# Inputs, expert rows and output in 4 KB runs per partition, and unread matmuls in TensorE's first idle time

## The reference

```python
def _fastmax_causal_p1(q, k, v):          # 16 heads of 64
    qn = jnp.max(jnp.linalg.norm(q, axis=-1), axis=-1)[..., None, None]
    kn = jnp.max(jnp.linalg.norm(k, axis=-1), axis=-1)[..., None, None]
    q = LIM * q / qn
    k = LIM * k / kn
    kv = jnp.cumsum(k[..., :, None] * v[..., None, :], axis=2)
    num = A0 * jnp.cumsum(v, axis=2) + A1 * jnp.einsum('bhnd,bhnde->bhne', q, kv)
    ksum = jnp.cumsum(k, axis=2)
    den = A0 * jnp.arange(1, n + 1) + A1 * jnp.einsum('bhnd,bhnd->bhn', q, ksum)
    return num / den[..., None]
# attention: vh @ Wo.T + bo
# experts: 8 of them, hidden width 352, top 2 per token, weights renormalised
acts = jax.nn.silu(gate) * up
expert_out = jnp.einsum('btef,efd->bted', acts, down_proj)
x = x + attention + jnp.einsum('bted,bte->btd', expert_out, expert_w)
```

## Time and profile before

| | |
|---|---|
| median of 3 runs | 1610.43 us (1609.39 to 1611.0) |
| profiled execution, its span | 1610.3 us |
| profiled execution, its own time | the span, with nothing else recorded around it: 0.13 us under the median |
| PE busy | 91% of the span |
| instructions | 39161 |
| DMA traffic | 53.44 MB, mean 33 GB/s |

### The profile page before, as it was taken

The page is one execution under the profiler, slowest core; times in us unless marked ns, Lnnn a source line. Parts: engine busy times, 40 slices in busy tenths (PEclk is TensorE's granted clock), DMA queues, the critical chain, the costliest instruction groups (busy, mean ns, idle before and its releaser), DMA issues.

```text
span 1610.3 us, 39161 instructions
## 1 busy us (share of the span) xinstructions
PE 1463.3 (91%) x9330; PEld 1317.9 (82%) x9332; DVE 1180.1 (73%) x3304; ACT 876.2 (54%) x2000; POOL 911.2 (57%) x1257
## 2 busy tenths in 40 slices
PE   2999975999999999999999999999998699999960
PEld 2999964888888888888888888888887699999960
DVE  7999997777777777777777777777777655555532
ACT  2999973555555555555555555555455444444430
POOL 3200016776776776776776776776676455555544
PEclk7999996999999999999999999999999899999985
DMA  9000000000000000000000000000000122222229
GB/s 289 19 0 0 0 1 14 12 11 8 11 11 8 11 11 8 11 11 8 11 11 8 11 11 8 11 11 8 10 11 7 42 63 62 61 63 62 59 65 291
DMA packets 72171, 53.44 MB, mean 33 GB/s; under 512 B 7840, under 2 KB 67360, under 8 KB 72096
## 3 DMA queue, kind: packets, MB, share of 16 engines
q1 hardware_dynamic: 54560, 28.95, 7.0%
q0 software_dynamic: 9216, 19.17, 3.4%
q10 hardware_dynamic: 8320, 4.19, 0.9%
HBM read 28.33 MB, written 23.96 MB: 32 GB/s over the span
## 4 chain that ended last, share of the span: by engine, by line
issue 31%; POOL 30%; PE 29%; POOLq 4%; DVE 3%; SPq 1%; DMA 1%; ACT 0%; DVEq 0%; ACTq 0%
POOL Al L414 11%; PE ybank L1248 6%; PE bank L1037 5%; PE bank L1039 5%; PE bank L1038 5%; POOL sorted_tokens L408 4%; POOL Ml L396 3%; POOL ysum L424 3%; PE ybank L1241 3%; POOL Mt L388 2%; POOL Mh L394 2%; SPq L331 1%; POOL xa L426 1%; PE ybank L1037 1%; PE ybank L1038 1%
## 5 line engine op out<-in xcount | busy, mean ns | idle before, releaser
L414 POOL TENSOR_TENSOR Al<-Am,Ah 128x512 fp32r<-128x512 f32 x256 | 329.4, 1287 | 177.7 <-ACT Ah L615 170.9
L615 ACT ACTIVATE Ah<-Am 128x512 fp32r<-128x512 f32 x256 | 161.5, 631 | 334.0 <-DVE Am L873 334.0
L1153 PE MATMUL ybank<-Wx,zf 128*128 128x129 f32 x2072 | 276.5, 276 | 4.8 <-ACT zf L620 4.8
L1153 PEld LDWEIGHTS ybank<-Wx,zf 128*128 128x128 f32 x2072 | 261.0, 191 | 22.3 <-issue 12.8
L866 DVE SCALAR_TENSOR_TENSOR ul<-bank,uh 128x512 fp32r<-128x512 f32 x256 | 174.0, 690 | 90.7 <-ACT uh L609 81.8
L898 DVE SCALAR_TENSOR_TENSOR acc<-ybank,rden,acc 128x128 f32<-128x128 f32 x780 | 217.7, 341 | 0.1
L504 POOL DMA_INDIRECT expert_rows<-yt,wdi x136 | 132.1, 972 | 142.0 <-ACT yt L687 121.5
L873 DVE TENSOR_TENSOR Am<-bank,causal 128x512 f32<-128x512 f32 x256 | 174.6, 682 | 23.1 <-PE bank L1039 23.1
L609 ACT ACTIVATE uh<-bank 128x512 fp32r<-128x512 f32 x256 | 148.7, 593 | 72.1 <-PE bank L1039 65.7
L786 DVE TENSOR_REDUCE ssq<-sq 128x448 f32 (+1 forms) x320 | 168.6, 573 | 7.6 <-ACT sq L557 5.8
L620 ACT ACTIVATE zf<-bank 128x512 f32<-128x512 f32 x258 | 151.7, 588 | 39.9 <-PE bank L1039 39.1
(11 more groups left out here) (225 smaller groups left out, 3906.2 us busy)
## 6 DMA issues: line engine op xcount, KB each, us to landing
xt<-sorted_tokens SPq DMA_DIRECT2D x137, 66.0 KB
er<-expert_rows SPq DMA_DIRECT2D x16, 512.0 KB, 8.5
xa<-in_L_attn_X SPq DMA_DIRECT2D x8, 512.0 KB, 7.3
out<-ot ACTq DMA_DIRECT2D x8, 512.0 KB, 7.1
expert_rows<-yt,wdi POOLq DMA_INDIRECT x136
sorted_tokens<-pay,sidx POOLq DMA_INDIRECT x128
gu<-in_L_ffn_gate_proj SPq DMA_DIRECT2D x1, 1408.0 KB
gu<-in_L_ffn_up_proj SPq DMA_DIRECT2D x1, 1408.0 KB
```

What stands on the lines that cost most here:

```text
L414: pool.tensor_tensor(Al[:, q], Am[:, q % 2], Ah[:, q], ALU.subtract).then_inc(e_Al, 1)
L615: act.activation(Ah[:, q], Am[:, q % 2], ACT.Copy).then_inc(e_Ah, 1)
L1153: last = pe.matmul(ybank[q % 2][:, i // 2, VE * (i % 2):VE * (i % 2) + VE], zf[:, q % 2, i, :], Wx[:, HQ * q + i, :], start=True, stop=True)
```

## The change

The host now lays out the inputs, and the kernel gives the output in another order, which the host turns back.

- x, wq, wk and wv come as [partition, tile, 128], so that each partition reads one run of 4 KB. `xa`, `wqn`, `wkn` and `wvn` hold the same values in the same places as before.
- gate and up come as one array, one run of 22 KB per partition and one DMA in place of two. The down weights come in two DMAs in place of sixteen, with `dn` laid out as [P, FT, E, D].
- `meta`'s destination rows change. The token in tile c of its batch at partition p now goes to row p*8 + c of the batch's block in `expert_rows`. The loads of `er` read the block with partition p taking rows 8p to 8p+7, a run of 4 KB. The scatters still write rows of 512 B, at other places.
- The output is [8, 128, 8, 128], a run of 4 KB per partition.
- PE gets `part_trials()` between the SETUP transpositions and its wait for their copies: 45 matmuls on zeros whose results nobody reads, some on 64 or 32 rows or columns of the array. POOL zeroes their two operands (2 memsets of 512 floats).

```diff
+        trial_r, trial_f = place("trial_r", [P, 4 * P], f32r), place("trial_f", [P, 4 * P])
...
-        dn = place("dn", [P, E, FT, D])
+        dn = place("dn", [P, FT, E, D])
...
             for n, (t, src) in enumerate(((wqn, wq), (wkn, wk))):
-                sp.dma_start(t[:], src.rearrange("(t p) d -> p t d", p=P)).then_inc(w_in[n], 16)
+                sp.dma_start(t[:], src).then_inc(w_in[n], 16)
             for n in range(8):
                 sp.dma_start(xa[:, 1 + n * CB:1 + (n + 1) * CB, :],
-                             x[n].rearrange("(c p) d -> p c d", p=P)).then_inc(x_in[n], 16)
-            sp.dma_start(wvn[:], wv.rearrange("(t p) d -> p t d", p=P)).then_inc(w_in[2], 16)
-            sp.dma_start(won[:], wo.rearrange("o (t d) -> o t d", d=D)).then_inc(w_in[3], 16)
+                             x[n]).then_inc(x_in[n], 16)
+            sp.dma_start(wvn[:], wv).then_inc(w_in[2], 16)
+            sp.dma_start(won[:], wo).then_inc(w_in[3], 16)
...
-            sp.dma_start(gu[:, :, 0, :], gate.rearrange("e d f -> d e f")).then_inc(f_w, 16)
-            sp.dma_start(gu[:, :, 1, :], up.rearrange("e d f -> d e f")).then_inc(f_w, 16)
+            sp.dma_start(gu[:], gate_up_w).then_inc(f_w, 16)
             sp.wait_ge(f_dz, 1)
-            for e in range(E):
-                sp.dma_start(dn[:, e, 0:2, :], down[e, 0:256, :].rearrange("(t p) d -> p t d", p=P)).then_inc(f_dn, 16)
-                sp.dma_start(dn[0:F - 256, e, 2, :], down[e, 256:F, :]).then_inc(f_dn, 16)
+            sp.dma_start(dn[:, 0:2], down_head).then_inc(f_dn, 16)
+            sp.dma_start(dn[0:F - 2 * P, 2], down_tail).then_inc(f_dn, 16)
...
-                        sp.dma_start(er[:, s, k], ys_d[bass.ds((b + B * k) * N, N), :].rearrange("(c p) d -> p c d", p=P)
+                        sp.dma_start(er[:, s, k], ys_d[bass.ds((b + B * k) * N, N), :].rearrange("(p c) d -> p c d", p=P)
...
-            pool.memset(dn[:, :, FT - 1, :], 0.0).then_inc(f_dz, 1)
+            pool.memset(dn[:, FT - 1], 0.0).then_inc(f_dz, 1)
+            pool.memset(trial_r[:].bitcast(f32), 0.0).then_inc(s_trial, 1)
+            pool.memset(trial_f[:], 0.0).then_inc(s_trial, 1)
...
-            pool.iota(meta[:, :, :, 0], pattern=[[P, C], [B * N, K2]], base=0, channel_multiplier=1,
+            pool.iota(meta[:].rearrange("p (b c) k m -> p b c k m", b=B)[:, :, :, :, 0],
+                      pattern=[[N, B], [1, CB], [B * N, K2]], base=0, channel_multiplier=CB,
...
-                    act.dma_start(out[bass.ds(b * CB, CB)].rearrange("c p d -> p c d"), ot[:, s]).then_inc(o_out[s], 16)
+                    act.dma_start(out[bass.ds(b, 1)].rearrange("a p c d -> p (a c) d"), ot[:, s]).then_inc(o_out[s], 16)
...
             for j, (kind, n) in enumerate(SETUP):
                 transpose4(bank[j], kind, n).then_inc(s_tr, 1)
+
+            def part_trials():
+
+                pe.wait_ge(s_trial, 2)
+                for n in range(6):
+                    pe.matmul(bank[4 + n % 4][:], trial_r[:, 0:P], trial_r[:], start=True, stop=True)
+                for n in range(6):
+                    pe.matmul(bank[4 + n % 4][:, 0:P], trial_r[:, 0:P], trial_r[:, 0:P], start=True, stop=True)
+                for rows in (64, 32):
+                    for n in range(8):
+                        t = slice(rows * n % P, rows * n % P + rows)
+                        pe.matmul(bank[4 + n % (P // rows)][:], trial_r[t, 0:P], trial_r[t, :], start=True, stop=True)
+                pe.matmul(bank[4][:], trial_f[:, 0:P], trial_f[:], start=True, stop=True)
+                for cols in (64, 32):
+                    for n in range(4):
+                        t = slice(cols * n % P, cols * n % P + cols)
+                        pe.matmul(bank[5][t, :], trial_f[:, t], trial_f[:], start=True, stop=True)
+                for n in range(4):
+                    r, c = slice(64 * (n % 2), 64 * (n % 2) + 64), slice(64 * (n // 2), 64 * (n // 2) + 64)
+                    pe.matmul(bank[6 + n % 2][c, :], trial_f[r, c], trial_f[r, :], start=True, stop=True)
+                for n in range(4):
+                    r = slice(64 * (n % 2), 64 * (n % 2) + 64)
+                    pe.matmul(bank[6 + n % 2][:, 0:P], trial_f[r, 0:P], trial_f[r, 0:P], start=True, stop=True)
+
+            part_trials()
             pe.wait_ge(s_trh, len(SETUP))
...
-            pe.wait_ge(f_dn, 32 * E)
+            pe.wait_ge(f_dn, 32)
```

More of the change, by code:

```diff
@@ L27 @@
+import numpy as np
 import concourse.bass as bass
@@ L52, with build @@
 EPS = 1e-5
-def build(nc, x, wq, wk, wv, wo, bo, rw, gate, up, down, out):
+def build(nc, x, wq, wk, wv, wo, bo, rw, gate_up_w, down_head, down_tail, out):
     f32, f32r, bf16 = mybir.dt.float32, mybir.dt.float32r, mybir.dt.bfloat16
@@ L195, in build @@
         s_stat, s_chain, s_rt, s_sqrt = sem("s_stat"), sem("s_chain"), sem("s_rt"), sem("s_sqrt")
-        s_rw = sem("s_rw")
+        s_rw, s_trial = sem("s_rw"), sem("s_trial")
         n_xn, n_xT, n_xTh, n_xTl = sem("n_xn"), sem("n_xT"), sem("n_xTh"), sem("n_xTl")
@@ L672, in _ @@
             barrier(act, 2)
-            act.wait_ge(f_w, 32)
+            act.wait_ge(f_w, 16)
             for e in (*range(E - 3, E), *range(E - 3)):
@@ L1247, in down_ @@
                 for t in range(FT):
-                    last = pe.matmul(bank[6 + s][:, 0:D], aT[:, s, t, :], dn[:, bass.ds(ex, 1), t, :].rearrange("p a f -> p (a f)"),
+                    last = pe.matmul(bank[6 + s][:, 0:D], aT[:, s, t, :], dn[:, t, bass.ds(ex, 1), :].rearrange("p a f -> p (a f)"),
                                      start=(t == 0), stop=(t == FT - 1))
@@ L1278, in _, with laid_out, a, by_partition @@
             barrier(pe, 3)
-_INS = ["L0_attn_X", "L0_attn_Wq", "L0_attn_Wk", "L0_attn_Wv", "L0_attn_Wo", "L0_attn_bo",
-        "L0_ffn_router_w", "L0_ffn_gate_proj", "L0_ffn_up_proj", "L0_ffn_down_proj"]
+def laid_out(inputs):
+    def a(name):
+        return np.asarray(inputs["L0_" + name])
+    def by_partition(w):
+        return w.reshape(8, P, D).transpose(1, 0, 2)
+    down = a("ffn_down_proj")
+    return {
+        "x": a("attn_X").reshape(B, CB, P, D).transpose(0, 2, 1, 3),
+        "wq": by_partition(a("attn_Wq")),
+        "wk": by_partition(a("attn_Wk")),
+        "wv": by_partition(a("attn_Wv")),
+        "wo": a("attn_Wo").reshape(D, 8, D),
+        "bo": a("attn_bo"),
+        "rw": a("ffn_router_w"),
+        "gate_up_w": np.stack([a("ffn_gate_proj"), a("ffn_up_proj")], axis=1).transpose(2, 0, 1, 3),
+        "down_head": down[:, :2 * P].reshape(E, 2, P, D).transpose(2, 1, 0, 3),
+        "down_tail": down[:, 2 * P:].transpose(1, 0, 2),
+    }
 def kernel(**inputs):
-    import numpy as np
     import concourse.bacc as bacc
@@ L1292 @@
     arrays, args = {}, []
-    for name in _INS:
-        a = np.ascontiguousarray(inputs[name])
+    for name, a in laid_out(inputs).items():
+        a = np.ascontiguousarray(a)
         arrays[f"in_{name}"] = a
         args.append(nc.dram_tensor(f"in_{name}", a.shape, mb.dt.from_np(a.dtype), kind="ExternalInput").ap())
-    args.append(nc.dram_tensor("out_0", (C, P, D), mb.dt.float32, kind="ExternalOutput").ap())
+    args.append(nc.dram_tensor("out_0", (B, P, CB, D), mb.dt.float32, kind="ExternalOutput").ap())
     build(nc, *args)
     r = run(nc, [arrays], core_ids=[0])
-    return r.results[0]["out_0"].reshape(B, N, D)
+    return np.ascontiguousarray(r.results[0]["out_0"].transpose(0, 2, 1, 3)).reshape(B, N, D)
```

## The result

The change makes the kernel slightly slower. The median is 1612.93 us (19 executions, 1610.29 to 1618.57) against 1610.05 us for the kernel before on the same chips (19 executions, 1608.23 to 1612.48): a ratio of 1.0018, 95% interval 1.0011 to 1.0026. The forecast was 1602.3 us, with a range of 1599.0 to 1606.5.

A forecast was written before the change was run, and what follows sets the result against it. DMA was taken to bound the last stage and DVE the first 33 us; -6.8 (output), -0.5 (last store), -0.8 (front) and 0 (trials) gave -8.1 us, 1602.3 us, range 1599.0 to 1606.5.

The forecast's parts named there:

- the trials at nothing: PE's first idle time: the 45 unread matmuls fit in 18.4 us of idleness and change the total by 0.
- The front: Start of the kernel: wqn's load lands earlier in larger packets, gaining 0.8 us, bounded by 0 and 1.5.
- DVE never waits again: Front: after wqn lands DVE works without a gap, so earlier landing of other loads gains nothing.
- the output stage: Last stage, DMA bound: 11.3 MB at 400 GB/s gains 6.8 us, the last store 0.5 us more.
- rival (2): Output stage: a data ceiling at 370 GB/s cuts the gain to 4.6 us, total 1604.6 us; chance 0.13.
- SP waiting for a buffer with the DMA idle: Output stage: a sign, named beforehand, that would show the forecast wrong; no size given.
- the round trip: Output stage: a buffer's adds, hand-overs and load take 10.6 us for four batches, so the DMA stays the bound.
- the scatters: Writes into expert_rows, now to rows eight apart: counted at nothing, from 0 to +2 us if the last landing doubles.
- full overlap of the trials: PE's first idle time: matmuls on different array parts run in parallel, taking 9.0 us and ending about 23 us.
- rival (1): First tile of the norms: the trials keep PE's clock up, -1.5 us more, 1600.8 us; chance 0.20.
- Rival (3): Output stage: no large packets, or the buffers' round trip binds; only the front gains, 1609.6 us; chance 0.06.
- (4): PE before the first tile: the trials run too long and hold PE back, 1624 us; chance 0.06.

The follow-up runs named there:

- e1: The changed kernel without the 45 unread matmuls, the memsets of their operands kept: 1606.76 us, ratio 0.9965 to the kernel before.
- e5: The changed kernel without the unread matmuls and without their two memsets, the new layouts alone: 1603.58 us, ratio 0.9953 to the kernel before.
- e8: The kernel before with only the output part added (er's read order, meta's rows, the store): 1605.09 us, ratio 0.9956 to the kernel before.
- e4: The changed kernel with 248 waits on a met semaphore (124 instructions) in place of the 45 matmuls: 1613.31 us, ratio 1.0018 to the kernel before.
- e2: The kernel before with only the 45 unread matmuls and their two memsets added: 1620.68 us, ratio 1.0058 to the kernel before.
- e9: The changed kernel with 80 waits on a met semaphore (40 instructions) behind the matmuls: 1606.07 us, ratio 0.9968 to the kernel before.
- e12: The new layouts alone, plus 80 unread matmuls run as a short PE loop in its first idle time: 1603.49 us, ratio 0.9965 to the kernel before.

## Why the prediction was wrong

**The failed step: the trials at nothing.** The prediction costed 45 matmuls by what they occupy (PE's idle 18.4 us) and named that as their cover. The cover held: they took 14.69 to 24.31 us, and the first tile waited on ACT. The price was elsewhere, in the room of 124 instructions in PE's program: 7.0 us at the three ways back in the profiled execution (0.08 to 7.06 us behind), of which 4.7 are standstills and most of the rest comes with the half clock behind the third; 8.5 us by the ratios of after and e1. I had given a chance only to trials that hold PE back (0.06), by their time; no rival moved code. The rows for it were in reach: "issue" three times in the waits of before, 2.3 us, each at a way back of a loop of 242 us.

**The front, mis-sized:** -0.8 us forecast, +0.4 us measured at the first tile and +0.1 at the start of the attention. The memsets were taken as hidden, because PE needs `ident` late. But they also push what POOL does next beneath DVE's centring, and there the engines slow each other: `ident`'s select took 1.13 us for 0.28, `meta`'s iota 0.96 us for 0.83, and DVE's small TENSOR_SCALAR of that moment 1.03 us, where in before's timeline it takes 0.17 (the select is in the earlier trace rows). Without the memsets (e5) that instruction took 0.52 us and the first tile came at 32.91 us, 0.43 before; so the memsets cost about 0.9 us there (e1 33.80, e5 32.91). But the step from the first tile to the total fails as well: of e5's lead 0.25 us are left at the third tile (39.81 against 40.06 us) and nothing at the first addition to Gf (282.48 against 282.46), where e1 stands at 282.49. So in before, after, e1 and e5 nearly nothing of what was gained or lost before the first tile reached the attention. In e8 a first tile 0.31 us early (33.03) became 0.6 us at the attention, with the clock back at 1.00 at 37.8 us where it is 38.6 in before and e5: what the front is worth hangs on the clock as well, which no run here takes apart. "DVE never waits again" was true, and beside the point: it can be slowed without waiting.

**Right: the output stage.** -6.6 us (e5 -6.5) against -6.8 and -0.5 forecast. GB/s is 381 from 1574.2 to 1601 us and 397 in the second half; the 400 I took was near, and rival (2), a ceiling at 370, is out. So is the 358 GB/s of the Trainium skill's "DMA: Bandwidth & Descriptors", section "Where 436 GB/s comes from", also for the loads of the front, 410 GB/s over 24 to 28 us. The full sum was missed by some 0.7 us. The dip shown above is of that size: about 1 us of transfer at the pace beside it, as an estimate from its three slices of 298, 146 and 228 GB/s. So the sign that the prediction had named, SP waiting for a buffer with the DMA idle, came in part: SP waits 4.4 us there, and in after the chain that ended last runs through two of POOL's adds (1580.37 to 1586.01 us) and one of DVE's (to 1590.38) before it is back at a load. The prediction had the round trip at 2.7 us a batch, below the DMA's 3.5; the adds, now partly side by side, take longer than it had reckoned. The rows of after, then of e5 (count, busy, mean ns, idle before):

```profile
L491 POOL TENSOR_TENSOR er<-er 128x1024 f32<-128x1024 f32 x8 | 21.2, 2661 | 16.4 <-DMA er<-expert_rows 16.4
L1002 DVE TENSOR_TENSOR ot<-er,xa 128x1024 f32<-128x1024 f32 x8 | 15.8, 1999 | 28.7 <-POOL er L491 28.7
```

```profile
L488 POOL TENSOR_TENSOR er<-er 128x1024 f32<-128x1024 f32 x8 | 21.5, 2692 | 16.1 <-DMA er<-expert_rows 16.1
L999 DVE TENSOR_TENSOR ot<-er,xa 128x1024 f32<-128x1024 f32 x8 | 9.8, 1226 | 34.5 <-POOL er L488 34.5
```

POOL's add alone takes 2.33 us (its first and last above), DVE's 1.23. Where they overlap, one of the two or both grow: in after three of DVE's take 3.2 to 3.4 us and POOL's reach 3.3; in e5 DVE's all stay at 1.23 and POOL's reach 3.4. POOL's waits are still all ended by er's landings, and e5's stage is as long as after's (38.1 against 38.0 us), so what the slower adds cost is not shown apart. The stage varies from 37.4 to 40.4 us between the profiles with the new order of expert_rows, which I did not resolve.

**Right: the scatters** at nothing; the gain of full overlap of the trials (9.6 us, forecast 9.0, end 24.3 for 23); and the clock, down at 28.1 us and so low for the first tile, so that rival (1) did not come. Rival (3) did not come. Of (4) the outcome came, slower, but not its mechanism: the trials held PE back by their place in the program, not by their time.

**The sum again:** +0.1 (up to the attention) + 7.0 (ways back) - 0.4 (from the third way back to the output) - 6.6 (output) = +0.1 us by the stretches of the two profiles, whose spans are equal to 0.1 us; the medians say +2.9. The difference is which executions were profiled: before's lies 2 us above its median, after's (1612.07 us) 0.9 us under it. After's executions reach from 1610 to 1619 us; the profiled kernels with the second standstill had half clock behind one way back (after, e4) and behind all three (e2), which may be part of that spread.

## What to carry to other kernels

An instruction on an idle engine is not free if a loop behind it is longer than what stays loaded (the sign here: packets on the instruction queue in every round). It moves the loop, and each way back may stand still once or twice, by all signs for code. Before judging an edit, look for waits on issue at the ways back, and when a small edit moves the time by more than its work, try it again with a few dozen empty instructions more. Work placed on POOL can slow DVE beside it (0.9 us at the first tile here) even where neither waits for the other; follow such a difference on before counting it, for here (e1 against e5) nothing of it was left at the attention.

## What the runs showed of the hardware

- A way back in a loop of some 15 packets of 16 KB of code costs PE 0.6 to 1.2 us where there is one standstill; with an unlucky head the two standstills are 1.9 to 3.0 us together (after, e2, e4). With shifts of 0, 65, 101, 164, 193 and 256 instructions there were three standstills, with 124 six.
- The granted clock fell to 0.50 for some 3.4 us behind all three ways back of e2 (second standstills of 1.58, 1.78 and 1.47 us) and behind the third of after and of e4 (1.74 and 1.48 us), with PE busy throughout. It stayed at 1.00 behind the other two of after (1.31, 1.20 us) and of e4, though those were 1.62 and 1.74 us. So the length of the second standstill does not decide it alone, and what does is open. Likewise every kernel has the wait of 2.60 us for POOL late in the attention: behind it the clock fell in before, after and most others, and stayed at 1.00 in e2, e4, e9 and e12.
- A wait on a met semaphore costs PE about 0.1 us an instruction (132 in 13.07 us).
- In after the loads of gate, up and down went at 410 GB/s over 24 to 28 us, in packets of 11 KB on average (1.64 MB in 149).
- DVE's add of 128x1024 took 1.23 us alone and up to 3.4 us beside POOL's (mean 2.00 in after); POOL's took 2.33 us alone and up to 3.4 us (mean 2.66 in after, 2.69 in e5, where DVE's stayed at 1.23).
- PE set off again 2.7 to 3.3 us after a 16 KB packet on the instruction queue at every way back of every profile, and 2.2 to 2.7 us after one in the second standstills.
